# Cross-attention with a routed feed-forward: the context packed at 96 rows for a batch, four batches in three blocks

## The reference, cut to what matters

```python
def _L0_xattn_ref(x, latents, mask, ...):        # x: the context (77 rows), latents: the 128 tokens
    x = layer_norm(x, ln_x_w, ln_x_b); latents = layer_norm(latents, ln_l_w, ln_l_b)
    q = latents @ Wq
    kv = concatenate([x, latents], axis=1) @ Wkv
    k, v = split(kv, 2, axis=-1)                 # 8 heads of 64
    q = l2norm(q) * q_scale; k = l2norm(k) * k_scale
    sim = where(full_mask, q @ k.T * 8, max_neg)
    out = softmax(sim) @ v
    return layer_norm(out @ Wo, ln_o_w, ln_o_b)
```

## Time and profile before

| | |
|---|---|
| median of three runs | 1005.2 us (1004.05 to 1006.25) |
| the profiled execution, its own time | 1005.38 us |
| its span, first to last instruction | 1003.6 us |
| mean granted TensorE clock | 0.990 of full speed |
| PE, PEld, DVE, ACT, POOL busy | 95%, 84%, 78%, 72%, 46% of the span |
| PE busy from 260 to 500 us | 238.0 of 240 us |
| four rounds (506.62 to 556.98 us) | 50.36 us |

### The profile page before, as it was taken

One profiled execution on the slowest core, in us unless ns is written; L12 is line 12 of the kernel. 1 busy time (PEld: TensorE's weight loads), 2 busy tenths in 40 slices (PEclk: granted clock), 3 DMA queues, 4 the chain that ended last, 5 costly groups with the idle time before them and its releaser, 6 DMA issues.

```text
span 1003.6 us, 31971 instructions
## 1 busy us (share of the span) xinstructions
PE 956.0 (95%) x10990; PEld 840.3 (84%) x10990; DVE 785.5 (78%) x2588; ACT 726.0 (72%) x1751; POOL 465.2 (46%) x1095
## 2 busy tenths in 40 slices
PE   3899999999999999999999999999999989899997
PEld 2788888888888888888888888888887778898997
DVE  4566788888888888888888888888888877877453
ACT  3778777777777777777777777777776665676564
POOL 5333333354545353535353535353535343877454
PEclk9899999999999999999999999999999998999999
DMA  7533000000000000000000000000000012245310
GB/s 208 172 102 64 2 2 2 2 13 2 13 1 11 0 11 0 11 0 11 0 11 0 11 0 11 0 11 0 11 1 10 4 40 68 58 94 106 90 45 22
DMA packets 49245, 30.51 MB, mean 30 GB/s; under 512 B 11066, under 2 KB 45821, under 8 KB 49165
## 3 DMA queue, kind: packets, MB, share of 16 engines
q1 hardware_dynamic: 43709, 19.93, 8.4%
q0 software_dynamic: 4320, 8.50, 2.8%
q10 hardware_dynamic: 1136, 1.05, 0.3%
HBM read 17.75 MB, written 12.17 MB: 30 GB/s over the span
## 4 chain that ended last, share of the span: by engine, by line
PE 80%; DVE 7%; ACT 4%; SPq 3%; issue 3%; POOL 1%; DMA 1%; DVEq 0%; POOLq 0%; ACTq 0%
PE ps L1525 13%; PE ps L1489 11%; PE ps L1287 7%; PE ps L1289 7%; PE ps L1466 7%; PE ps L1288 7%; PE ps L1565 7%; PE ps L1444 5%; PE ps L1452 5%; PE ps L1551 3%; PE ps L1544 2%; SPq L421 2%; SPq L422 2%; DVE sumsq L1189 1%; PE ps L1326 1%
## 5 line engine op out<-in xcount | busy, mean ns | idle before, releaser
L1189 DVE TENSOR_REDUCE sumsq<-qk_hat 128x8 f32<-128x512 f32 x192 | 123.1, 677 | 35.3 <-ACT qk_hat L522 35.2
L1525 PE MATMUL ps<-qT_all,kT_all 64*128 64x128 f32 x2048 | 148.7, 285 | 2.1 <-ACT w_all L531 1.2
L1489 PEld LDWEIGHTS ps<-v_sb,prob 128*64 128x64 f32 x4096 | 128.8, 138 | 25.0 <-issue 13.8
L1489 PE MATMUL ps<-v_sb,prob 128*64 128x65 f32 x4096 | 143.8, 224 | 5.9 <-ACT qq_t L571 2.4
L1221 DVE TENSOR_TENSOR qk_hat<-ps,rstd 128x512 f32<-128x512 f32 x192 | 120.6, 684 | 29.7 <-POOL rstd L749 27.9
L580 ACT ACTIVATE prob<-ps,neg_shift 128x512 f32<-128x512 f32 x128 | 88.7, 693 | 74.5 <-PE ps L1525 74.5
L1525 PEld LDWEIGHTS ps<-qT_all,kT_all 64*128 64x128 f32 x2048 | 124.2, 187 | 20.9 <-ACT prob L580 15.1
L1287 PE MATMUL ps<-w_hi,xc_hi 128*128 128x512 f32 x320 | 138.7, 433 | 2.4 <-POOL xc_lo L716 2.4
L522 ACT ACTIVATE qk_hat<-ps 128x512 f32<-128x512 f32 x192 | 113.3, 599 | 32.4 <-PE ps L1289 21.8
L742 POOL TENSOR_TENSOR rs_t<-rs_y 128x32 f32<-128x32 f32 x73 | 17.6, 241 | 245.4 <-ACT rs_y L559 245.4
L1289 PE MATMUL ps<-w_hi,xc_lo 128*128 128x512 f32 x320 | 126.7, 396 | 0.0
(11 more groups left out here) (233 smaller groups left out, 2138.0 us busy)
## 6 DMA issues: line engine op xcount, KB each, us to landing
x_res<-sorted_rows SPq DMA_DIRECT2D x71, 65.5 KB, 1.9
w_all<-in_L_ffn_W_dram SPq DMA_DIRECT2D x16, 256.0 KB, 4.7
x_res<-in_x_dram SPq DMA_DIRECT2D x5, 768.0 KB
sorted_rows<-fill SPq DMA_DIRECT2D x8, 327.5 KB, 7.2
ctx_res<-in_ctx_dram SPq DMA_DIRECT2D x5, 462.0 KB
out_dram<-prob,x_res POOLq DMA_INDIRECT x71, 2.4
sorted_rows<-stage,idx POOLq DMA_INDIRECT x64, 2.4
sorted_rows<-fill SPq DMA_DIRECT2D x1, 524.0 KB, 4.9
```

Of the source, the lines that this page charges most:

```text
L1189: nc.vector.reduce_sum(sumsq[:, n * H:(n + 1) * H], sq[:, n * INNER:(n + 1) * INNER].rearrange("p (h d) -> p h d", d=DH), AX).then_inc(ss_ ...
L1489: last = nc.tensor.matmul(dst[half:half + DH, :], prob[:, kt, at + half:at + half + DH], v_sb[:, 1 - par, kt, h, :], start=kt == 0, stop=k ...
L1525: last = nc.tensor.matmul(ps_s[2 * kt + half][:, cols], k_t[rows, kt, cols], q_t[rows, cols], start=True, stop=True)
```

## The change

A batch's context takes 96 rows of a dense array in place of 128, so four batches fill three blocks of 128 rows: batch p of a lap of four begins at row 96 p. Block 0 holds batch 0 (rows 0 to 76) and the first 32 rows of batch 1, block 1 the rest of batch 1 and 64 rows of batch 2, block 2 the rest of batch 2 and batch 3. `fresh(pos)` is true in the first round that needs a block (p = 0, 1, 2), and false for p = 3. Layer norm, projections, transposes, squares, sums and copies of the context are done for a block and not for a batch. So for p = 3 there are none, and for the other three they run over 128 rows where the transposes and their copies ran over 77.

- The scores of the context's keys of batches p = 1 and 2 take two blocks: each of the 8 matmuls becomes two, of 64 rows by 64 columns of the array. Batches 0 and 3 lie in one block.
- v of the context is kept in `v_c`, one buffer for each p; what a batch needs of a block that lies in another's buffer is copied by VectorE (`MOVES`, three copies of 64 partitions by 512 in a lap, at the end of the round), and TensorE waits for them (`v_moved`) before `weighted`.
- The masks of the keys are loaded packed in the same way, in 6 DMAs (3 on SP, 3 on ACT) in place of one. A lot's context is loaded in up to 6 DMAs in place of one (2 for lot 0, 4 for lot 1); the last lots have 24 batches. Batch 1 needs block 1, which comes with lot 1. Expert 3's weights are asked for ahead of lot 2.
- The second attention transposes three blocks in place of four contexts (line 1359), and `ctx_now` has three blocks.
- The experts' `h_t` has four buffers in `k_t` and no longer one pair in `prob`, so a wait at its tile 2 goes.

```diff
@@ rounds
-            with eng.Fori(0, LOOP_TURNS) as turn:
-                for n in range(4):
-                    run(LOOP_FROM + 4 * turn + n, n % 2, n, (LOOP_FROM - 2) // 4 - 1 + turn, True)
+            with eng.Fori(0, LOOP_ROUNDS // LAP) as turn:
+                for n in range(LAP):
+                    pos = LOOP_FROM + n
+                    run(pos + LAP * turn, n % 2, n % 4, (pos - 2) // 4 - 1 + LAP // 4 * turn, True, pos, turn)
@@ SyncE
-                sp.dma_start(ctx_res[0:M, lot, :], ctx[lot].rearrange("b m d -> m b d")).then_inc(ld_lot[n], 16)
+                for to, src in context_pieces(packed[n]):
+                    sp.dma_start(to, src).then_inc(ld_lot[n], 16)
...
+            sp.wait_ge(mask_zeroed, 1)
+            for to, src in itertools.islice(mask_pieces(), ON_SP):
+                sp.dma_start(to, src).then_inc(ld_w, 16)
             arrived(0)
@@ ScalarE
-                    for kt in (0, 1):
+                    for kt in (0, 1) if fresh(pos) else (0,):
...
-                    for n in range(3):
+                    for n in range(3) if fresh(pos + 1) else range(2):
                         act.wait_ge(qk_done, 3 * j + 4 + n)
...
-                        for n, rows in enumerate((P, M)):
-                            last = nc.scalar.activation(xc_t[:, par, n, 0:rows], ps_xc[:, n * P:n * P + rows], ACT.Identity,
+                        for n in (0, 1) if fresh(pos + 2) else (0,):
+                            last = nc.scalar.activation(xc_t[:, par, n, :], ps_xc[:, n * P:(n + 1) * P], ACT.Identity,
@@ VectorE
+                    if fresh(pos + 3):
+                        dve.wait_ge(blocks_in, block_of(pos + 3, turn) + 1)
+                        dve.sem_inc(s["fence_v"], 1)
+                        nc.vector.bn_stats(bn6[:, 1, :], one(ctx_res, block_of(pos + 3, turn)))
...
+                if has(j, inside) and fresh(pos):
+                    block = FRESH[pos % LAP]
+                    dve.wait_ge(v_copied, 2 * j + 2)
+                    dve.sem_inc(s["fence_v"], 1)
+                    for half, p in MOVES[block]:
+                        rows = slice(half * DH, (half + 1) * DH)
+                        nc.vector.tensor_copy(v_c[rows, p % 4, :, 0:DH], v_c[rows, HOME[block] % 4, :, 0:DH]).then_inc(v_moved, 1)
@@ TensorE
-                    for n in range(3):
+                    for n in range(3) if fresh(pos) else range(2):
...
-                    for kt in (0, 1):
+                    for kt in (0, 1) if fresh(pos) else (0,):
                         last = product(ps_v[kt], xc_hi[:, par, kt, :], xc_lo[:, par, kt, :], 2 * INNER)
...
+                    pe.wait_ge(v_moved, moves_by(pos - 1, turn))
                     weighted(range(H // 2, H))
...
+                            if kt == 0 or halves(pos)[0] == halves(pos)[1]:
+                                keys = k_t[rows, 0 if kt == 0 else kept(halves(pos)[0]), cols]
...
+                            else:
+                                for key, n in zip((0, DH), halves(pos)):
+                                    keys = k_t[rows, kept(n), t * P + key:t * P + key + DH]
+                                    last = nc.tensor.matmul(ps_s[2 * kt + half][key:key + DH, cols], keys, q_t[rows, cols],
+                                                            start=True, stop=True)
```

More of the change, by code:

```diff
@@ L1 @@
+import itertools
 import math
@@ L35 @@
 G = 4
[L37 removed]
+LOOP_FROM, LOOP_ROUNDS = 18, 40
 AHEAD = 3
@@ L43 @@
 DEEP = 6
+STEP = 96
+ON_SP = 3
 STORES = 8
@@ L221, in whole @@
         g_small = ps[:, 3, 0:G * E]
-        lots = [slice(0, 2), slice(2, 4)] + [slice(n, min(n + 12, B)) for n in range(4, B, 12)]
+        lots = [slice(0, 2), slice(2, 4), slice(4, 16), slice(16, 40), slice(40, B)]
+        ends = [1, 3] + [STEP * lot.stop // P for lot in lots[2:]]
+        packed = [slice(lo, hi) for lo, hi in zip([0] + ends, ends)]
         ld_lot = [sem(f"ld_lot{n}") for n in range(len(lots))]
@@ new lines, in whole @@
+        for n in range(BLOCKS):
+            FRESH[min(p for p in range(LAP) if n in halves(p))] = n
+            HOME[n] = ([p for p in range(LAP) if halves(p) == (n, n)] + [p for p in range(LAP) if halves(p)[1] == n])[0]
+            MOVES[n] = [(half, p) for p in range(LAP) for half in (0, 1) if halves(p)[half] == n and p != HOME[n]]
+            PIECES[n] = []
+            for p in range(LAP):
+                lo, hi = max(STEP * p, P * n), min(STEP * p + M, P * n + P)
+                if lo < hi:
+                    PIECES[n].append((p, lo - P * n, hi - P * n, lo - STEP * p, hi - STEP * p))
@@ new lines, in whole, with fresh, block_of, moves_by @@
+        for p in range(LAP):
+            if halves(p)[0] != halves(p)[1]:
+                assert STEP * p % P >= DH and (STEP * p + M) % P <= DH
+        def fresh(pos):
+            return pos % LAP in FRESH
+        def block_of(pos, turn):
+            return BLOCKS * (pos // LAP) + FRESH[pos % LAP] + BLOCKS * turn
+        def moves_by(pos, turn):
+            return (pos // LAP + turn) * sum(map(len, MOVES.values())) + sum(len(MOVES[n]) for p, n in FRESH.items() if p <= pos % LAP)
+        def kept(n):
+            return 1 + n % 3
@@ L1127, in first_weights, with run @@
                         nc.vector.tensor_copy(w, ps[:, bank, :]).then_inc(s["w_taken"], 1)
-            def run(j, par, rho, g, inside=False):
+            def run(j, par, rho, g, inside, pos, turn):
                 if has(j - 3, inside):
@@ L1223, in run @@
                                                 rstd[:, par, n * H:(n + 1) * H].unsqueeze(2).to_broadcast([P, H, DH]),
-                                                ALU.mult).then_inc(scaled, 1)
+                                                ALU.mult).then_inc(scaled, 1 if n == 0 or fresh(pos + 1) else 2)
                 if has(j + 3, inside):
-                    for n, res in enumerate((x_res, ctx_res)):
-                        last = nc.vector.tensor_scalar(xc_hat[:, 1 - par, n, :], one(res, j + 3),
+                    rows = [one(x_res, j + 3)] + ([one(ctx_res, block_of(pos + 3, turn))] if fresh(pos + 3) else [])
+                    for n, row in enumerate(rows):
+                        last = nc.vector.tensor_scalar(xc_hat[:, 1 - par, n, :], row,
                                                        xc_stat[:, 1 - par, n, 0:1], rstd[:, par, 24 + n:25 + n],
```

186 lines of the change are left out of this document (106 added, 80 removed).

## The result

The changed kernel takes 989.8 us (median of four runs, 989.56 to 990.63), the kernel before 1004.6 us beside it (1003.99 to 1006.25): a ratio of 0.985, 95% interval 0.9832 to 0.9869. Forecast were 993.6 us with 986 to 1003, so the sign and the range held; the gain is 14.8 us where 11.8 were forecast.

The account below looks back on a forecast made before the run. TensorE's queue was taken to bound the kernel. From its own time of 1005.4 us, -12.2 for 16 laps and +0.5 for the start gave 993.7, stated as 993.6 us against the median, range 986 to 1003.

Parts of the forecast that it names:

- the lap's term: Lap of four rounds: -0.96 us on TensorE, +0.1 and +0.1 for others, -0.76; times 16, -12.2 us.
- What bounds the kernel: Whole kernel: TensorE's queue is full, so its time is kernel time, costed by distances between starts.
- the removal: Context's k and v products (1.38 us), key transposes (0.26) and one of `xc_hat` (0.065) go: 1.71 us a lap.
- What comes, 0.75 us a lap, and 0.1 for ScalarE's wider copy: Wider transposes, 0.68 in fresh rounds and 0.07 in the second attention; ScalarE's `xc_t` copy, 0.1, ahead of `o_t`.
- The split scores at 0: `scores(1)`, rounds p = 1 and 2: quarters overlap as halves do, +0; upper bound +0.9 us.
- Round p = 3 and its second chain: `v_s` before line 1544 comes 0.91 us earlier, TensorE 0.95; line 1352 waits for `o_c`; about 0.1 us, once.
- VectorE's copies at 0: Three copies into `v_c`, 0.46 us each, ending rounds p = 0, 1, 2: covered, cost 0; uncovered 1.4 us a lap.
- one of the signs of being wrong: TensorE showing holes before lines 1352, 1544 or 1489 (`v_moved`) whose releaser is VectorE.
- Start +0.5: Start: context in two DMAs, an issue taking 0.47 us, delays the first normalisation by 0.5 us; range 0 to +2.
- Rounds: Round rho = 1 near 12.0 us, rho = 0 about 0.5 shorter, the other two 0.1 to 0.2 longer.
- Sixteen equal laps: All 16 laps (64 batches) lie in the bound stretch, so the lap's -0.76 us counts 16 times.
- VectorE takes over: Rival: VectorE's copies and chain through `o_c`, sums and `v_s` stop TensorE next round; 998 to 1015 us, chance 0.12.

Follow-up runs that it names:

- e10: Kernel before with only the removal: every fourth batch without context work, blocks 77 wide, no copies, no quarters; 981.8 against 1004.6 us, ratio 0.9777.
- e5: Kernel before with its context's transposes and their two evictions over 128 rows and columns in place of 77, all 64 rounds; 1035.5 against 1027.0 us, ratio 1.0096.
- e1: Changed kernel with the second score product in quarters in every round, not only two of four; 1008.3 us, ratio 0.9841.
- e8: Changed kernel with two small VectorE instructions earlier: `sinv` ahead of the sums of squares, `place` between them; 1008.3 us, ratio 0.9824.
- e4: Changed kernel with VectorE's three copies, inside the loop, moving 4 of the 64 columns of each head; 1010.2 us.
- e3: Changed kernel with an extra VectorE sum over as many values (0.67 us) ahead of each of the three copies; 1018.5 us, ratio 0.9936.
- e11: e8 with all three copies moved behind the statistics of the output product in the next round; 988.9 against 1004.6 us, ratio 0.985.
- e9: Kernel before, unedited, run again for its trace; 1006.4 us in its one run.
- e0: Changed kernel again, unedited, on the chip of e1, e3 and e4; 1011.0 us, ratio 0.986.

## Why the prediction was right, step by step

The forecast was 11.8 us and the gain 14.8. The rounds from 1 on gave 13.7, where the lap's term gave 12.2; another 1.8 came from the clock in round 0, for which the prediction had no term. That part is luck.

- *What bounds the kernel.* Right in the main: with distances between TensorE's starts as the price, the removal came to 1.54 us in e10 where 1.61 were forecast (1.71 less the 0.1 for the chain through `v_s` and `o_c`). But a distance can hold a wait: from the second score product to the product with Wo TensorE follows ScalarE in three rounds of four (e5).
- *What comes, 0.75 us a lap, and 0.1 for ScalarE's wider copy.* This is the step that was mis-sized. It measures 0.55 (e10 against the changed kernel), though 0.04 of that are the quarters', costed at nothing. The keys' transposes cost what I took, 0.17 a round, but 0.04 of it come back in the line behind them in two of the three rounds. The fifth, of `xc_hat`, fills a wait for ScalarE's exponential. The second attention's transposes cost 0.02 where 0.07 were taken. ScalarE's wider copy is seen by the path that the prediction named, through `o_t`, 0.04 us a round in rounds p = 0 and 2; in p = 1 only one copy of `xc_t` is left, and TensorE doesn't wait there. The lap is -1.54 + 0.55 = -0.99, where -0.76 were forecast.
- *The split scores at 0.* Right to 0.04 us a lap, shown by e1 and e10. The 1.14 us that I took for eight instructions on halves held 0.05 of waiting for `o_t`; without it they take 1.09 (e10), and the quarters take 1.03 but start 0.09 later. 32 records on quarters, 16 on either row half, take 1.03 us, while the weight load of each lasts 133 ns, so those of one row half would take 2.1 us one after the other. By the rule of the Trainium skill, "TensorE: Matmul & The Clock Gate", section "The mechanism", that a weight load overlaps only in another row group, they would have; the trace disagrees.
- *Round p = 3 and its second chain.* Right in kind: the round went to 11.91 where 12.0 were forecast, with a hole of 0.18 before line 1636. The other place, line 1352 waiting for `o_c`, showed only in e8.
- *VectorE's copies at 0.* Right in the steady laps, shown by e4; e3 and e11 show how thin the cover is. One of the three takes 0.84 us and not 0.46 (at 522.04, beside GpSimd's `xc_lo`; that of p = 2 ran beside it too and took 0.41, so the cause is open); that is covered too. A hole whose releaser is VectorE, one of the signs of being wrong, did appear before line 1573, but it hangs on `place` and not on a copy, and costs 0.15 us.
- *Start +0.5.* Its reason failed. With two traces of the kernel before, the changed start is within 0.1 us of it (24.90 and 24.97 for round 0). What did change, by -1.8 us between rounds 0 and 1, is the clock, which the prediction took as it was.
- *Rounds.* Forecast: p = 2 shorter by 0.5, p = 0 and 1 longer by 0.1 to 0.2. Seen: 0.40, 0.14 and 0.16.
- *Sixteen equal laps.* Not so in the first two, and there the rival "VectorE takes over" holds in part. From round 0 to 4 the lap gains 0.33 us beyond the clock's 1.80, from round 4 to 8 0.30 us in place of 0.99, and e10's removal 1.14 in place of 1.54. TensorE's rounds are shorter there (round 7 took 10.89 us before, and takes 10.84), VectorE is busy 10.0 of the 10.8 us of round 7, and TensorE of the changed kernel waits for it once, while the kernel before has no such wait. The wait, in the stretch from 73.5 to 117.8 us:

```profile
PE ps L1642 <- DVE o_n L1285: 0.9, 1, 0.9
```

Left open: what took the half clock away. It is gone with wider blocks (e5) and with less work (e10) alike, so no single part of the change explains it; e5 ran on chip 15, where the unedited kernel before was not traced, e10 on the chip of e9. No experiment here varied the start alone.

## What to carry to other kernels

Where TensorE's queue is full, price a change by distances between starts in the trace, and compare each start with the end of what it needs from another engine: TensorE had no hole ahead of `scores(1)` and the product with Wo, yet both started 0.05 us after an instruction of ScalarE had ended, so a wider transpose ahead of them was free and a wider copy on ScalarE was not. An instruction on an engine that is three quarters busy is free or not by its place: a copy of 64 x 512 cost nothing at the end of one round, 0.2 us at the end of another once a wait ahead of it was gone, and 0.24 us at the head of the next. After a change has shortened one engine's rounds, look at each small wait that is left and at the shortest instruction that ends it; moving two of them and one copy was worth nearly half as much as the whole change. And don't multiply one steady lap by all laps: the first two gained a third of it.

## What the runs showed of the hardware

- Matmuls of 64 rows by 64 columns, four to a pass, run side by side: 32 records in 1.03 us, 0.032 us each, while one lasts 269 ns and its load 133 ns.
- TensorE's clock fell to 1.2 GHz from about 25 to 32 us (granted 0.50 and 0.55 of full speed from 25 to 26 us) in both traces of the unedited kernel before and in no other. Ahead of it, from 14 to 24 us, TensorE was busy 7.2 and 7.0 of 10 us in those two, and 7.15 in the changed kernel and 7.3 in e10, so the busy time ahead doesn't tell them apart.
- VectorE's copy of 64 x 512 between SBUF tiles took 0.41 us in most places, 0.84 at the end of round p = 0, 0.64 in e8 and 1.28 in e11. Beside `xc_lo` of GpSimd it took 0.41 in one place and 0.84 in another, so that instruction alone doesn't explain it.
- The same programs took some 21 us more in one set of runs than in the other, nearly all of it after round 63. TensorE in e0, then in the changed kernel:

```profile
900.00:950.00 50.00, 40.78 (x301) 38.98 (x301) 25.33 (x100) 22.57 (x86) 22.97 (x24) 0.86 0.37 79
```
```profile
900.00:950.00 50.00, 47.09 (x401) 46.23 (x401) 29.79 (x112) 30.78 (x117) 26.55 (x27) 0.97 0.29 77
```

A quarter fewer matmuls in the same 50 us, at a lower clock. The rounds before agree to 0.02 us a lap. What makes the experts' part slower there was not tried.
